# Linear attention in a graph layer: high and low halves side by side in one stationary operand

## The reference, cut to what matters

```python
def _fourier_kernel(x, proj_mat):
    p = jnp.einsum('blhd,dm->blhm', x, proj_mat) / math.sqrt(D_HEAD)
    return jnp.concatenate([jnp.cos(p), jnp.sin(p)], axis=-1) / math.sqrt(D_KMAP)
q = (x2 @ wq + bq).reshape(B, L, N_HEAD, D_HEAD)
k = (x2 @ wk + bk).reshape(B, L, N_HEAD, D_HEAD)
v = (x2 @ wv + bv).reshape(B, L, N_HEAD, D_HEAD)
qp = _fourier_kernel(q, proj_mat)
kp = _fourier_kernel(k, proj_mat)
kv = jnp.einsum('blhm,blhd->bhmd', kp, v)
attn = jnp.einsum('blhm,bhmd->blhd', qp, kv)
```

## Time and profile before

| | |
|---|---|
| median of 3 runs | 1334.69 us (1333.11 to 1338.66) |
| the profiled execution | 1334.61 us, its span 1332.8 us |
| PE busy in the span | 1247.7 us (94%) |
| DVE | 766.2 us (57%) |
| ACT | 631.6 us (47%) |
| POOL | 340.5 us (26%) |
| linear attention in the span | about 155 to 710 us |
| mean granted clock of PE | 0.971 of full speed |

### The profile page before, as it was taken

How to read it: one execution, slowest core, us unless ns; L and a number is a source line. 1 busy time by engine, 2 the same in 40 slices (tenths; PEclk the granted TensorE clock), 3 DMA queues, 4 the chain that set the end, 5 groups by cost and what they waited for, 6 DMA issues and landing times. The chain is left out here.

```text
span 1332.8 us, 19542 instructions
## 1 busy us (share of the span) xinstructions
PE 1247.7 (94%) x7017; PEld 1088.1 (82%) x7017; DVE 766.2 (57%) x1212; ACT 631.6 (47%) x917; POOL 340.5 (26%) x296
## 2 busy tenths in 40 slices
PE   6989889999999999999957999799999999899997
PEld 4556689999999999999946787699997887788874
DVE  7979625455655556565553376577774321556546
ACT  8175534555555555555554533332233442455544
POOL 1400003241423232332220201056662433021000
PEclk9999999999999999999976999899999799999999
DMA  8011310111020202020214645432335232620112
GB/s 207 10 29 25 78 36 1 33 35 54 12 66 0 66 0 66 0 66 0 67 45 150 216 151 172 137 107 81 92 91 192 74 93 62 211 72 14 50 32 93
DMA packets 72193, 99.41 MB, mean 75 GB/s; under 512 B 27241, under 2 KB 52165, under 8 KB 71631
## 3 DMA queue, kind: packets, MB, share of 16 engines
q1 hardware_dynamic: 68684, 86.11, 22.5%
q0 software_dynamic: 3456, 12.58, 3.1%
HBM read 77.04 MB, written 21.63 MB: 74 GB/s over the span
## 5 line engine op out<-in xcount | busy, mean ns | idle before, releaser
L1140 POOL TENSOR_TENSOR cos_sin_lo<-cos_sin,cos_sin_hi 125x1024 fp32r<-125x1024 f32 (+1 forms) x40 | 95.8, 2396 | 351.2 <-ACT cos_sin_hi L1214 351.2
L1201 ACT ACTIVATE cos_sin<-part_turn 125x512 f32<-125x512 f32 (+1 forms) x80 | 50.1, 627 | 152.7 <-DVE part_turn L1329 152.7
L468 PE MATMUL p_cnt<-hot_s,hot_d 125*125 125x418 bf16 x540 | 113.8, 361 | 1.8 <-DVE hot_d L401 1.8
L705 PE MATMUL p_h<-x 128*125 128x512 f32 x400 | 109.3, 400 | 0.0
L399 DVE TENSOR_SCALAR hot_s<-iota_h,ends 125x1250 bf16<-125x1250 f16 x180 | 98.2, 546 | 14.6 <-PE p_cnt L468 12.5
L468 PEld LDWEIGHTS p_cnt<-hot_s,hot_d 125*125 125x125 bf16 x540 | 63.3, 140 | 51.6 <-DVE hot_d L401 40.6
L1414 PE MATMUL p_w<-x,mix_hi_v 128*128 128x416 f32 (+1 forms) x384 | 105.2, 355 | 0.0
L1414 PE MATMUL p_w<-x,mix_hi_k 128*128 128x416 f32 (+1 forms) x384 | 104.2, 352 | 0.0
L1414 PE MATMUL p_w<-x,mix_hi_q 128*128 128x416 f32 (+1 forms) x384 | 104.1, 352 | 0.0
L966 PE MATMUL rows_in_psum<-h_hi,a_lo 125*125 125x342 f32 x300 | 96.8, 323 | 3.0 <-DVE a_lo L910 3.0
L1327 DVE TENSOR_SCALAR whole_turns<-p_p 125x512 f32<-125x512 f32 (+1 forms) x80 | 54.4, 680 | 77.0 <-PE p_p L1465 74.4
(11 more groups left out here) (302 smaller groups left out, 3169.8 us busy)
## 6 DMA issues: line engine op xcount, KB each, us to landing
x_in<-in_x_dram SPq DMA_DIRECT2D x30, 448.0 KB
attn_dram<-attn_t SPq DMA_DIRECT2D x8, 625.0 KB, 3.9
at_in<-attn_dram SPq DMA_DIRECT2D x10, 500.0 KB, 4.6
x_rows<-in_x_dram SPq DMA_DIRECT2D x10, 448.0 KB
x_in<-gnn_dram SPq DMA_DIRECT2D x10, 448.0 KB
out_dram<-rows SPq DMA_DIRECT2D x10, 448.0 KB
mix_in_v<-in_L_mix_wv_dram SPq DMA_DIRECT2D x8, 512.0 KB, 6.0
mix_in_k<-in_L_mix_wk_dram SPq DMA_DIRECT2D x8, 512.0 KB, 4.7
```

What stands on the lines that cost most here:

```text
L468: last = pe.matmul(p_cnt[0:T, t % 2, n, 0:w], hot_d[:, j, 0:T], hot_s[:, j, a:a + w], start=False, stop=False)
L705: last = pe.matmul(p_h[0:T, i % 2, n, :], left[i % 2][:, k, :], right[:, k, cols], start=(k == 0 and m == 0), stop=(k == K8 - 1 and m == 2))
L1140: pool.tensor_tensor(full(cs_lo, k), full(cs, k), f32(full(cs_hi, k)), ALU.subtract).then_inc(s_cslo[0], 1)
L1201: act.activation(step_view(cs, k, 1), rows(part, k), ACT.Sin, scale=TWO_PI)
```

## The change

The high and low parts of the values stand side by side in one tensor `v_both` (tile, head, part, 64 columns), and a stationary operand is the high and the low half of one head's values, 64 and 64 columns. A matmul takes the 256 columns of that head only, once with the low and once with the high part of the cosines and sines. The result has the product with the high values in partitions 0 to 63 and that with the low values in 64 to 127, for each head in a bank of its own; low times low is now part of the sum. The two partition halves are added when the result is kept: after the transposes they lie in columns, so ACT copies one half to `kv_sum` and DVE adds the other (`add_kv`). `kv_both` holds high and low of the sums side by side in the same way, and the attention comes out in two partition halves as well: ACT copies the high ones to `attn_t` in two instructions of 64 partitions, and DVE adds the others (`add_attention`), after which `s_atk` is raised. `p_at` is now the second bank of `p_kv`, so the first accumulation of a pair waits for the last addition of the pair before. `copy_kv` stands ahead of `phases(j, 6)` instead of behind it, and the value run around the transposes is cut after 3 instead of 4 of its 8 steps. Two POOL memsets at the stage's start are gone.

```diff
-        v_hi = sb("v_hi", [T, NT, 128], F32R)
-        v_lo = sb("v_lo", [T, NT, 128], F32R)
+        v_both = sb("v_both", [T, NT, 2, 2, DH], F32R)
...
-        kv_hi = sb("kv_hi", [128, 4, 128], F32R)
-        kv_lo = sb("kv_lo", [128, 4, 128], F32R)
+        kv_sum = sb("kv_sum", [128, 4, DH])
+        kv_both = sb("kv_both", [128, 4, 2, DH], F32R)
...
-        p_kv = ps("p_kv", [128, 512])
-        p_at = ps("p_at", [128, 512])
+        p_kv = ps("p_kv_at", [128, 2, 512])
+        p_at = p_kv[:, 1]
...
             def keep_kv(j):
                 act.wait_ge(s_tr, 4 * j + 4)
+                act.activation(kv_sum[:], p_tr[:, :, DH:2 * DH], ACT.Copy, scale=1.0 / KMAP).then_inc(s_kvs, 1)
+                act.wait_ge(s_kvs, 2 * j + 2)
                 for h in range(2):
-                    last = act.activation(kv_hi[:, 2 * h:2 * h + 2, h * DH:(h + 1) * DH],
-                                          p_tr[:, 2 * h:2 * h + 2, h * DH:(h + 1) * DH], ACT.Copy, scale=1.0 / KMAP)
+                    last = act.activation(kv_both[:, 2 * h:2 * h + 2, h], kv_sum[:, 2 * h:2 * h + 2], ACT.Copy)
                 last.then_inc(s_trhi, 1)
...
             def keep_attention(j, c):
                 act.wait_ge(s_at, STEPS * j + c + 1)
-                act.activation(attn_t[:, c * CHUNK:(c + 1) * CHUNK], p_at[:, 0:CHUNK], ACT.Copy).then_inc(s_atk, 1)
+                for h in range(2):
+                    head = slice(h * DH, (h + 1) * DH)
+                    last = act.activation(attn_t[head, c * CHUNK:(c + 1) * CHUNK], p_at[head, h * CHUNK:(h + 1) * CHUNK], ACT.Copy)
+                last.then_inc(s_atc, 1)
...
+            def add_kv(j):
+                dve.wait_ge(s_kvs, 2 * j + 1)
+                dve.scalar_tensor_tensor(kv_sum[:], p_tr[:, :, 0:DH], 1.0 / KMAP, kv_sum[:], ALU.mult, ALU.add).then_inc(s_kvs, 1)
...
             def keep_kv(j):
                 dve.wait_ge(s_trhi, 4 * j + 4)
                 for h in range(2):
-                    last = dve.scalar_tensor_tensor(kv_lo[block_h], p_tr[block_h], 1.0 / KMAP, f32(kv_hi[block_h]),
-                                                    ALU.mult, ALU.subtract)
+                    last = dve.tensor_tensor(kv_both[:, 2 * h:2 * h + 2, 1 - h], kv_sum[:, 2 * h:2 * h + 2],
+                                             f32(kv_both[:, 2 * h:2 * h + 2, h]), ALU.subtract)
                 last.then_inc(s_trlo, 1)
+            def add_attention(j, c):
+                dve.wait_ge(s_atc, STEPS * j + c + 1)
+                for h in range(2):
+                    head, other = slice(h * DH, (h + 1) * DH), slice((1 - h) * DH, (2 - h) * DH)
+                    here = attn_t[head, c * CHUNK:(c + 1) * CHUNK]
+                    last = dve.tensor_tensor(here, here, p_at[other, h * CHUNK:(h + 1) * CHUNK], ALU.add)
+                last.then_inc(s_atk, 1)
...
             def accumulate_kv(j, k):
                 if k == 0:
                     pe.wait_ge(s_kvt, j)
+                    pe.wait_ge(s_atk, STEPS * j)
...
-                    for m, (left, right) in enumerate(((v_lo, hi), (v_hi, lo), (v_hi, hi))):
-                        last = pe.matmul(p_kv[:], left[:, 2 * k + i, :], right[:, i].rearrange("p h c m -> p (h c m)"),
+                    for m, right in enumerate((lo, hi)):
+                        for h in range(2):
+                            last = pe.matmul(p_kv[:, h, 0:2 * KMAP], v_both[:, 2 * k + i, h].rearrange("p a d -> p (a d)"),
+                                             right[:, i, h].rearrange("p c m -> p (c m)"),
...
                 for b in range(4):
-                    for m, (left, right) in enumerate(((kv_lo, cs_hi), (kv_hi, cs_lo), (kv_hi, cs_hi))):
-                        last = pe.matmul(p_at[:, 0:CHUNK], left[:, b, :], right[:, k % 2, cols],
+                    h = b // 2
+                    for m, right in enumerate((cs_lo, cs_hi)):
+                        last = pe.matmul(p_at[:, h * CHUNK:(h + 1) * CHUNK], kv_both[:, b].rearrange("p a d -> p (a d)"),
+                                         right[:, k % 2, b * CHUNK:(b + 1) * CHUNK],
...
                 if more:
-                    value_run(j + 1, 2, 0, half)
+                    value_run(j + 1, 2, 0, half - 1)
                 transpose_kv(j)
                 if more:
-                    value_run(j + 1, 2, half, K8)
+                    value_run(j + 1, 2, half - 1, K8)
```

More of the change, by code:

```diff
@@ L1054, in linear_attention @@
         s_kvt = core.sem("kv_copied")
+        s_kvs = core.sem("kv_halves_added")
+        s_atc = core.sem("attention_high_kept")
         s_at = core.sem("attention_in_psum")
@@ L1185, in keep_v @@
                 act.wait_ge(s_tr, 4 * j + group + 1)
-                act.activation(v_hi[:, first:first + count, :], p_tr[0:T, 0:count, :], ACT.Copy).then_inc(s_trhi, 1)
+                act.activation(v_both[:, first:first + count, :, 0], p_tr[0:T, 0:count, :].rearrange("p i (h d) -> p i h d", h=2), ACT.Copy).then_inc(s_trhi, 1)
             def keep_kv(j):
                 act.wait_ge(s_tr, 4 * j + 4)
+                act.activation(kv_sum[:], p_tr[:, :, DH:2 * DH], ACT.Copy, scale=1.0 / KMAP).then_inc(s_kvs, 1)
+                act.wait_ge(s_kvs, 2 * j + 2)
                 for h in range(2):
-                    last = act.activation(kv_hi[:, 2 * h:2 * h + 2, h * DH:(h + 1) * DH],
-                                          p_tr[:, 2 * h:2 * h + 2, h * DH:(h + 1) * DH], ACT.Copy, scale=1.0 / KMAP)
+                    last = act.activation(kv_both[:, 2 * h:2 * h + 2, h], kv_sum[:, 2 * h:2 * h + 2], ACT.Copy)
                 last.then_inc(s_trhi, 1)
@@ L1311, in keep_v @@
                 dve.wait_ge(s_trhi, 4 * j + group + 1)
-                dve.tensor_tensor(v_lo[:, first:first + count, :], p_tr[0:T, 0:count, :],
-                                  f32(v_hi[:, first:first + count, :]), ALU.subtract).then_inc(s_trlo, 1)
+                dve.tensor_tensor(v_both[:, first:first + count, :, 1], p_tr[0:T, 0:count, :].rearrange("p i (h d) -> p i h d", h=2),
+                                  f32(v_both[:, first:first + count, :, 0]), ALU.subtract).then_inc(s_trlo, 1)
+            def add_kv(j):
+                dve.wait_ge(s_kvs, 2 * j + 1)
+                dve.scalar_tensor_tensor(kv_sum[:], p_tr[:, :, 0:DH], 1.0 / KMAP, kv_sum[:], ALU.mult, ALU.add).then_inc(s_kvs, 1)
             def keep_kv(j):
@@ L1344, in copy_kv @@
                 dve.wait_ge(s_added, STEPS * (j + 1))
-                dve.tensor_copy(kv_t[:], p_kv[:].rearrange("p (b m) -> p b m", b=4)).then_inc(s_kvt, 1)
+                dve.tensor_copy(kv_t[:].rearrange("p (h c) m -> p h (c m)", h=2), p_kv[:, :, 0:2 * KMAP]).then_inc(s_kvt, 1)
             for which in (KEY, QUERY):
@@ L1475, in accumulate_kv @@
                 for i in range(2):
-                    for m, (left, right) in enumerate(((v_lo, hi), (v_hi, lo), (v_hi, hi))):
-                        last = pe.matmul(p_kv[:], left[:, 2 * k + i, :], right[:, i].rearrange("p h c m -> p (h c m)"),
-                                         start=(k == 0 and i == 0 and m == 0), stop=(k == STEPS - 1 and i == 1 and m == 2))
+                    for m, right in enumerate((lo, hi)):
+                        for h in range(2):
+                            last = pe.matmul(p_kv[:, h, 0:2 * KMAP], v_both[:, 2 * k + i, h].rearrange("p a d -> p (a d)"),
+                                             right[:, i, h].rearrange("p c m -> p (c m)"),
+                                             start=(k == 0 and i == 0 and m == 0), stop=(k == STEPS - 1 and i == 1 and m == 1))
                 last.then_inc(s_added, 1)
@@ L1486, in attend @@
                 for b in range(4):
-                    cols = slice(b * CHUNK, (b + 1) * CHUNK)
-                    for m, (left, right) in enumerate(((kv_lo, cs_hi), (kv_hi, cs_lo), (kv_hi, cs_hi))):
-                        last = pe.matmul(p_at[:, 0:CHUNK], left[:, b, :], right[:, k % 2, cols],
-                                         start=(b == 0 and m == 0), stop=(b == 3 and m == 2))
+                    h = b // 2
+                    for m, right in enumerate((cs_lo, cs_hi)):
+                        last = pe.matmul(p_at[:, h * CHUNK:(h + 1) * CHUNK], kv_both[:, b].rearrange("p a d -> p (a d)"),
+                                         right[:, k % 2, b * CHUNK:(b + 1) * CHUNK],
+                                         start=(b % 2 == 0 and m == 0), stop=(b % 2 == 1 and m == 1))
                 last.then_inc(s_at, 1)
```

15 lines of the change are left out of this document (9 added, 6 removed).

## The result

The change made the kernel slower: 1349.11 us (median, 1345.11 to 1351.19) against 1334.17 for the kernel before on the same chip, ratio 1.0102, 95% interval [1.0074, 1.0131]. The forecast was 1338.6. The time lies inside the range of 1319 to 1351, near its upper end, and outside the forecast's own range of 1331 to 1342. It goes with the chance "slower" (0.30), not with the forecast's "same".

What follows compares the result with a forecast made beforehand. PE (TensorE), busy 94% of the span, was taken to bound the kernel. Terms by pair and clock, -0.8 - 2.0 + 5 x 0.3 + 1.8 + 3.5 = +4.0, gave 1338.6 us, range 1319 to 1351.

Steps and rivals of the forecast that it cites:

- slower: Chance 0.30 that the change makes the kernel slower, by the clock.
- same: The forecast itself, 1338.6 us, with its own range of 1331 to 1342; chance 0.43.
- pair 0: First pair of heads, up to its first attend: PE's gain stays, 5 x 0.43 - 1.4 = 0.8 us.
- pair 1: Second pair of heads: slack of 4.1 us at the fourth accumulation, so PE's gain stays, 2.0 us.
- pairs 2 to 6: PE is let in 0.9 us early at the fourth accumulation, the key-value chain takes 1.4; +0.3 us a pair.
- the last pair: No value or key run fills PE, and the next stage's weight splits come later: +1.8 us, bounds -1 and +3.
- PE's saving: Each accumulation 0.43 us and each attend 0.47 us shorter on PE: 4.5 us a pair, 36 us in eight pairs.
- The copy moved ahead of `phases(6)`: After the last accumulation: the copy costs nothing, and PE's 0.52 us idle before the transposes of `kv_t` goes.
- The key-value chain: Last accumulation to first attend: added copy, addition and POOL-held subtractions make the attend 1.4 us later, PE waiting 2.1 us.
- Rival 1: Chains bind less: POOL does not hold the subtractions, or two DVE instructions pass ahead of POOL; 1324 to 1327 us, 20%.
- The clock: The new wait of 2.1 us before the first attend drops PE's clock in two of seven pairs: +3.5 us.
- Rival 3: Slower, by the clock: it falls once in each of seven pairs, +12 instead of +3.5 us: 1347 us, 30%.

Runs made afterwards that it cites:

- e2: Changed kernel with the added key-value sum written back to PSUM, so ACT's copy and DVE's two subtractions read PSUM; 1338.24 us, ratio 1.0019.
- e5: Changed kernel with the sum kept in PSUM and without the two DVE additions behind each attend; 1319.81 us, ratio 0.9879.
- e11: Changed kernel; in the last pair alone DVE splits two parts of the next stage's weights before the additions for the fifth attend; 1346.95 us, ratio 1.0086.
- e12: Changed kernel with one edit: SP issues the next pair's key weights before the store of the attention; 1343.5 us, ratio 1.0072.
- e10: Changed kernel with sum in PSUM, `query_phases(7)` before the first attend, key weights before the store, two last-pair weight splits before the last additions; 1327.68 us, ratio 0.9944.
- e3: Changed kernel without the two DVE additions behind each attend; 1337.48 us, ratio 0.9999.
- e7: Changed kernel without the additions, with eight unused matmuls of 416 columns put into PE's wait before the first attend; 1327.45 us, ratio 0.9941.
- e1: Kernel before with two products in place of three in accumulations and attends, nothing added; 1311.07 us, ratio 0.981.
- e9: Accumulations alone side by side, attends as before, `query_phases(7)` ahead of the first attend, key weights issued before the store; 1315.15 us, ratio 0.986 to the kernel before.
- e4: One half of the change alone: accumulations side by side, attends as in the kernel before, no additions behind them; 1325.52 us, ratio 0.9909.

## Why the prediction was right and wrong, step by step

The forecast was +4.0; the start of the next stage came 11.0 later: pair 0 -3.0 for -0.8, pair 1 +1.3 for -2.0, pairs 2 to 6 +5.3 for +1.5, the last pair +5.9 for +1.8, one fall of the clock +1.5 for +3.5. That the time lies in the stated range owes much to the range's width: most terms missed, and mostly in one direction.

**PE's saving: right in kind, 3.9 us a pair for 4.5.** 0.12 us for 250 or 256 columns held; the longer first matmul of an attend and the 1.02 to 1.06 of an accumulation did not stand in the sum.

**The copy moved ahead of `phases(6)`: right**, the wait for `kv_t` is gone.

**The key-value chain: right.** The attend starts 7.68 behind the end of the last accumulation (7.83 forecast), PE waits 1.82 (2.1), POOL holds the subtractions (e2).

**Pair 0** came out at 0.9 earlier for 0.8 (the other 2.1 of 3.0: the stage began 0.6 earlier, and the clock did not fall at the first accumulation, 1.5).

**Pair 1: wrong by 3.3 us.** The forecast read a slack of 4.1 us off it and let PE keep 2.0 (its terms, 4.5 less 1.4, give 3.1; where the rest goes it doesn't say); the pair took 1.3 longer. Part of the slack was not room but a race that DVE had won. `phases(3)` and `phases(4)` of pair 1 on DVE, POOL beside them, before and then after:

```profile
269.79 0.69 DVE L1332 SCALAR_TENSOR_TENSOR whole_turns<-part_turn 125x512 f32<-125x512 f32 x1
...
275.16 0.69 DVE L1332 SCALAR_TENSOR_TENSOR whole_turns<-part_turn 125x512 f32<-125x512 f32 x1
...
270.47 2.41 POOL L1136 TENSOR_TENSOR mix_lo_k<-mix_in_k,mix_hi_k 128x1024 fp32r<-128x1024 f32 x1 [7.08 <-ACT mix_hi_k L1171]
```

```profile
268.05 2.24 DVE L1349 SCALAR_TENSOR_TENSOR whole_turns<-part_turn 125x512 f32<-125x512 f32 x1
...
274.69 2.80 DVE L1349 SCALAR_TENSOR_TENSOR whole_turns<-part_turn 125x512 f32<-125x512 f32 x1
...
267.35 2.40 POOL L1137 TENSOR_TENSOR mix_lo_k<-mix_in_k,mix_hi_k 128x1024 fp32r<-128x1024 f32 x1 [6.97 <-ACT mix_hi_k L1172]
```

Before, DVE's third instruction starts 0.68 ahead of POOL's split and takes 0.69. After, it starts 0.70 behind the split's start: 2.24, and the next one 2.80. A shift of 1.4 us between the two engines cost DVE 3.7. Rival 1 had named this race only the other way round.

Two things made the shift. Against the first attend of pair 0, DVE's instruction comes 1.28 us later (36.73 for 35.45); e2 and e5, which differ by the additions alone, have it at 36.67 and 34.70. And the key weights, issued later in the pair, took 4.44 us from issue to ACT's split instead of 5.97. In e11, the same program up to here, they took 5.97 again, and DVE won with the additions in place:

```profile
271.21 0.69 DVE L1349 SCALAR_TENSOR_TENSOR whole_turns<-part_turn 125x512 f32<-125x512 f32 x1
...
276.74 0.69 DVE L1349 SCALAR_TENSOR_TENSOR whole_turns<-part_turn 125x512 f32<-125x512 f32 x1
...
272.05 2.42 POOL L1137 TENSOR_TENSOR mix_lo_k<-mix_in_k,mix_hi_k 128x1024 fp32r<-128x1024 f32 x1 [8.52 <-ACT mix_hi_k L1172]
```

That pair of e11 took 66.34, 1.57 of them a fall of the clock: without it 64.8, 0.9 less than the 65.67 of the changed kernel's profile and still 2.4 more than forecast. So the lost race is worth about 0.9 of the 3.3 us. The larger part is there without it, as in pairs 2 to 6.

**Pairs 2 to 6: wrong in size, +1.06 a pair instead of +0.3** (without the one fall of the clock). The term was the additions for the fourth and fifth attend. At `keep_lo(9)` DVE is 1.02 ahead of before, as forecast (1.14), and the fourth attend waited 0.66, as forecast too. But at `phases(0)` it is 0.02 ahead, not 0.48: the pair of additions takes 0.84, not 0.74, and does not overlap; with its hand-overs it pushes 1.00 where 0.66 was put. With the second pair the store comes 29.04 behind the first attend (28.2 forecast, 27.63 before), and `keep_lo(4)` ends at 56.50 for 55.7, as much too late. The waits stand before the third accumulation (1.00) and the fourth attend (0.66); at the fifth accumulation, where the forecast had its sum, PE starts 0.05 behind the end of `keep_lo(4)`. The chain was the right one as far as runs show it: e12 takes its weights' link out and gets back about what was expected. The link that stays is the one argued at e10.

```profile
382.88 1.19 DVE L1353 TENSOR_TENSOR cos_sin_lo<-cos_sin,cos_sin_hi 128x1000 fp32r<-128x1000 f32 x1
384.11 0.84 DVE L1337 TENSOR_TENSOR attn_t<-attn_t,p_kv_at 64x250 f32<-64x250 f32 x2
384.98 0.69 DVE L1344 TENSOR_SCALAR whole_turns<-p_p 125x512 f32<-125x512 f32 x1
...
390.40 0.84 DVE L1337 TENSOR_TENSOR attn_t<-attn_t,p_kv_at 64x250 f32<-64x250 f32 x2
...
416.58 2.41 POOL L1141 TENSOR_TENSOR cos_sin_lo<-cos_sin,cos_sin_hi 125x1024 fp32r<-125x1024 f32 x1 [8.85 <-ACT cos_sin_hi L1216]
```

**The last pair: wrong, +5.9 instead of +1.8 (bounds -1 and +3).** The forecast moved only the last splits. It left out that the additions are a link in each of four rounds of attend, addition, attend, where PE has no run to fill the time, and that the splits queued behind them free the buffers for SP's next transfers:

```profile
702.22 3.35 DVE L1357 TENSOR_TENSOR x<-mix_in_q,x 128x1024 fp32r<-128x1024 f32 x1
...
705.63 1.06 ACT L1223 ACTIVATE x<-mix_in_k 128x1024 fp32r<-128x1024 f32 x1 [2.69 <-DMA mix_in_k<-in_L_gnn_W_dram]
...
713.45 1.06 ACT L1223 ACTIVATE x<-mix_in_v 128x1024 fp32r<-128x1024 f32 x1 [1.94 <-DMA mix_in_v<-in_L_gnn_W_dram]
...
718.99 1.22 DVE L1357 TENSOR_TENSOR x<-mix_in_k,x 128x1024 fp32r<-128x1024 f32 x1
```

ACT waits 2.69 and 1.94 us for weights (1.90 and 0.33 before), one split is held by POOL to 3.35 us, and the last split starts at 718.99, 11.0 later than the earlier trace rows. Without additions (e3, e5, e7) the last stretch is 29.1, before 28.96: they are the whole cause of its 5.3 us.

**The clock: overestimated** in the profile, one fall for two; e11, the same program up to the last pair, had three. Rival 3 gave 1347, close to the measured time, but by seven falls; its number is right for another reason. Waits of 1.8 us did bring the clock down in other kernels, six times of seven in e3. The forecast's mechanism was that the other engines' chains take nearly all that PE saves. e1 shows what they take when nothing is added, 1.2 of 4.2 us a pair, and e9 that PE waits for nothing once they are mended; with the change's own additions they took more than all. The forecast underrated the links that the change itself adds to those chains.

## What to carry to other kernels

When PE's work shrinks, count each instruction added on another engine as a link of the ring that goes round once per loop, with its duration, its hand-over and the transfers queued behind it, and not as idle time used. An early margin between two engines that hold each other up may be a race won and not slack: ask what a delay of one microsecond, or a transfer that lands sooner, turns round. A change with two halves is worth timing as halves: here the one gives 0.9% (1.4% with two more mends around it), and the other, added to it, costs more than it saves with the mends (e10) and without them.

## What the runs showed of the hardware

- The hold between DVE and POOL works both ways. POOL's split takes 2.41 us; where DVE's instruction with both operands in SBUF had started 0.30 ahead of it (e9, 386.72 and 387.02), it took 3.19.
- The same wait of 1.82 us before the same matmuls left the clock at 1.00 in six of seven pairs of the changed kernel and let it fall in six of seven of e3; in e11 it fell in three of seven, in e12 in one. What else decides it, these runs don't show. Behind waits of 0.84 us and less (e2, e4 to e7, e10) it never fell at that place.
- Two DVE additions of 250 elements on 64 partitions each take 0.84 together, 0.42 each, where two subtractions of 128 elements on all partitions take 0.49.
- The first matmul of an attend that waited takes 0.22 us (0.19 before the fourth attend) where the next ones take 0.12. The list of waits doesn't explain it alone: the first matmuls of the second, third and fifth attend, before which no wait is listed, take 0.19 to 0.20.
- The same three weight transfers, issued in the same order behind the store, had the key weights ready for ACT 4.4 to 6.0 us after their issue (4.44 and 5.97 in two profiles of the same program at the same place).
